# Narrow score tiles of an attention kernel share a PSUM bank and an exponential, and products with V are taken two steps at a time

## The chip, the cores and the metric

The kernel runs on one core of one Trainium2 chip. The metric is the time of one execution on the device, in microseconds (us); every time without a unit in this document is in us. TensorE (PE) multiplies matrices into PSUM, a buffer of 8 banks of 512 fp32 values in each of 128 partitions; ScalarE (ACT) computes exponentials and copies; VectorE (DVE) reduces and adds; GpSimd (POOL) cannot read PSUM and here masks and adds in SBUF; SyncE (SP) issues most transfers.

## The reference

A layer of attention and a layer of a mixture-of-depths feed-forward, each followed by a layer normalisation. Batch 8, 1024 tokens, width 512, 16 heads of 32.

```python
qkv = encodings @ W_attn + b_attn
scores = jnp.einsum('bhki,bhqi->bhkq', k, q) / math.sqrt(HEAD)
mask = jnp.arange(n)[:, None] <= jnp.arange(n)[None, :]
scores = jnp.where(mask, scores, jnp.float32(-10000.0))
attn = jax.nn.softmax(scores, axis=2)
combined = jnp.einsum('bhkq,bhkl->bhql', attn, v)
out = combined.transpose(0, 2, 1, 3).reshape(b, n, HIDDEN) @ W_out + b_out
...
x = _layernorm(x + _L0_attn_ref(x, ...))
x = _layernorm(x + _L0_ffn_ref(x, ...))     # top half of the tokens by score, gelu, scattered back
```

The softmax runs over the key positions `k` that are not after the query position `q`, which makes the scores a triangle.

## The kernel before

The attention part is cut into 64 **units**: for each of 8 batches and 4 groups of 4 heads, the first 512 queries (an even number u, the narrow unit) and the last 512 (an odd number, the wide unit). Two units are a **pair**; there are 32, four to a batch. Each unit passes over its scores twice. Pass A (`a_piece`, line 1287) takes the scores with queries on the partitions, and VectorE (lines 948 and 956) finds the maximum of each query. It is then carried in two extra rows of Q (line 1294 turns the maxima round), so that pass B gives scores that have it subtracted.

Pass B (`b_tile`, line 1318) takes the scores with 128 keys on the partitions: a **step** k is 128 keys, 4 steps in a narrow unit and 8 in a wide one. On the diagonal a step has only the queries from its own keys on, so the last four steps of a unit are 512, 384, 256 and 128 queries wide (`width`). "Step 35.6" below is step 6 of unit 35, which is 256 wide, and 35.7 is 128 wide. A step is four score tiles, one for each head (a to d: 35.3d is the fourth), each in a PSUM bank of its own; two banks, 3 and 4, take turns, so tile j waits until the exponential of tile j-2 has run (semaphore `b_exp`). ScalarE takes one exponential for each tile (line 851) into a buffer of the step: step 0 goes to `acc` (`Pa` in the profile), the others in turn to one of three, `Pm` (two) and `P3` (`P`). From there:

- GpSimd masks the triangle of a diagonal step (line 719, semaphore `keep`) and adds the step to `acc` (line 732, semaphore `padd`); `acc` in the end holds what the sums over all keys are made of. It takes the steps strictly in order.
- TensorE multiplies the step with V (`pv`, line 1334): four heads, each with 32 weight columns and its own 32 output partitions. It waits for the exponentials and, on the diagonal, for `keep`. This is the **product** of the step. `sums`/`N` (line 1261) is a product of the same form that adds `acc` up over the partitions, once in a unit; ScalarE turns it into a reciprocal by a logarithm and an exponential (lines 886 and 888).
- The exponentials of a step wait until the product and the addition of the step three before it are done, since they share its buffer.

Between the tiles TensorE does "dense" work: the projections to K and Q (line 1238) and V (line 1246) for later units, the output projection (line 1252) for earlier tokens. The order is written by a table of **beats** (class `Table`): 32 beats to a pair. Tiles of pass A, tiles of pass B, pieces of dense work and products each have a place in time, and on every engine the order within a beat follows. The table gives the tiles of a unit their places in proportion to a cost for each tile (`168 + 0.87 * width`), and the products of step k a beat two or three behind the one in which the step is formed; the products of the last two steps of a unit stand together. On ScalarE, the copies of projected K and Q (line 869, `nat`) and the conversion of attention outputs (line 895, `Os`) stand behind the exponentials of their beat.

After the attention part the feed-forward runs alone, some 835 us (lines 1368 and 1385); no edit touches it.

## Time and profile before

| | us |
|---|---|
| median of 3 runs | 2638.15 (2637.4 to 2640.35) |
| the profiled execution's own time | 2636.7 |
| its span, first to last instruction | 2634.9 |
| PE with a matmul in flight | 2526.2 (96%) |
| PE loading weights | 1810.5 (69%) |
| DVE busy | 1737.9 (66%) |
| POOL busy | 1518.8 (58%) |
| ACT busy | 1230.9 (47%) |

Times in the profile count from the start of the span. A matmul's record goes from its start to the arrival of its last column and overlaps the next one's, so what a matmul costs is read from start to start. An fp32 product appears as two records for each head, so a step's product is a row of eight. Names in a row are "output<-inputs" without buffer numbers. The mean granted TensorE clock is 0.982.

### The profile page before, as it was taken

The numbers are of one execution on the slowest core, as the hardware profiler recorded it, in microseconds if no ns is written. First come the engines' busy times: TensorE is split into PE (matmuls) and PEld (weight loads), VectorE is DVE, ScalarE is ACT, GpSimd is POOL, SyncE is SP. The second block draws the span as 40 slices with busy tenths as digits, with TensorE's granted clock in tenths as the row PEclk, the third lists the DMA queues.
The fourth block names the chain that finished last, engine by engine and source line by source line (L and its number), as shares of the span: only waits on it lengthen the run. The fifth ranks groups of instructions, "written<-read, shape, count | busy, mean of one in ns | idle before, by whom it ended". The sixth has DMA issues, their size and how long they took to land.

```text
span 2634.9 us, 40165 instructions
## 1 busy us (share of the span) xinstructions
PE 2526.2 (96%) x13920; PEld 1810.5 (69%) x13920; DVE 1737.9 (66%) x4224; ACT 1230.9 (47%) x2342; POOL 1518.8 (58%) x1229
## 2 busy tenths in 40 slices
PE   5999999999999999999999999998899999999997
PEld 4566666666666666666667666665588888888885
DVE  5757678777777877777787677777465435643532
ACT  1555565566565566665565665565631111111110
POOL 0566787687788777778777777876331213122311
PEclk8999999999999999999999999998999999999998
DMA  6766557676666767656666575764431011001000
GB/s 172 127 113 127 101 129 161 125 156 138 137 137 124 164 134 149 154 113 145 126 162 144 124 167 116 141 135 129 160 102 36 25 33 41 17 25 41 29 20 16
DMA packets 167931, 289.57 MB, mean 110 GB/s; under 512 B 23153, under 2 KB 58033, under 8 KB 166578
## 3 DMA queue, kind: packets, MB, share of 16 engines
q1 hardware_dynamic: 160562, 270.15, 47.4%
q0 software_dynamic: 7168, 16.85, 2.0%
q8 instruction: 112, 1.84, 0.3%
q14 instruction: 89, 0.73, 0.1%
HBM read 120.11 MB, written 65.11 MB: 70 GB/s over the span
## 4 chain that ended last, share of the span: by engine, by line
PE 81%; DVE 6%; ACT 4%; POOL 3%; DMA 3%; issue 2%; SPq 1%; ACTq 0%; DVEq 0%; POOLq 0%
PE PS L1385 13%; PE PS L1368 13%; PE PS L1238 10%; PE PS L1318 10%; PE PS L1334 9%; PE PS L1287 9%; PE PS L1252 7%; PE PS L1246 7%; POOL Pa L732 3%; PE PS L1261 2%; DVE xTl L1046 2%; DMA Qp<-nat 1%; DMA h_s<-hs 1%; DVE nm L948 1%; ACT Pm L851 1%
## 5 line engine op out<-in xcount | busy, mean ns | idle before, releaser
L732 POOL TENSOR_TENSOR Pa<-Pa,Pm 128x1024 f32<-128x1024 f32 (+2 forms) x332 | 704.3, 2137 | 168.7 <-ACT Pm L851 119.3
L1318 PE MATMUL PS<-Qp,Kp 98*128 98x512 f32 (+3 forms) x1536 | 548.0, 361 | 16.3 <-ACT P L851 4.6
L851 ACT ACTIVATE Pm<-PS 128x512 f32<-128x512 f32 (+3 forms) x856 | 397.1, 471 | 336.0 <-PE PS L1318 319.7
L1287 PE MATMUL PS<-Kp,Qp 96*128 96x512 f32 (+3 forms) x1536 | 503.9, 363 | 37.8 <-DMA Qp<-nat 18.2
L948 DVE TENSOR_REDUCE nm<-PS 128x1 f32<-128x512 f32 x512 | 345.5, 686 | 223.8 <-PE PS L1287 223.2
L1318 PEld LDWEIGHTS PS<-Qp,Kp 98*128 98x128 f32 x1536 | 293.0, 192 | 220.8 <-ACT Pm L851 92.8
L732 POOL TENSOR_TENSOR Pa<-Pa,P 128x1024 f32<-128x1024 f32 (+2 forms) x164 | 349.3, 2145 | 78.6 <-ACT P L851 55.4
L1287 PEld LDWEIGHTS PS<-Kp,Qp 96*128 96x128 f32 x1536 | 284.0, 194 | 117.3 <-issue 32.5
L820 ACT ACTIVATE G<-PS,b1c 128x512 f32<-128x512 f32 x128 | 88.2, 689 | 539.6 <-PE PS L1368 520.6
L956 DVE CUSTOM_DVE_ANT_0 PS<-PS,maskA 128x384 f32<-128x384 f32 (+3 forms) x512 | 245.3, 505 | 143.5 <-PE PS L1287 141.8
L1385 PE MATMUL PS<-W2h,Gs 128*128 128x512 f32 x1024 | 316.6, 390 | 0.9 <-DVE W2l L1051 0.9
L956 DVE CUSTOM_DVE_ANT_0 PS<-PS,maskA,nm 128x384 f32<-128x384 f32 (+3 forms) x512 | 260.7, 552 | 41.6 <-PE PS L1287 38.4
L1368 PE MATMUL PS<-hT,W1h 128*128 128x512 f32 x1024 | 271.9, 389 | 0.0
L851 ACT ACTIVATE P<-PS 128x512 f32<-128x512 f32 (+3 forms) x424 | 196.6, 469 | 158.3 <-PE PS L1318 148.7
L1098 DVE CAST Gs<-G 128x512 fp32r<-128x512 f32 x128 | 54.4, 425 | 310.1 <-ACT G L820 239.3
L1368 PEld LDWEIGHTS PS<-hT,W1h 128*128 128x128 f32 x1024 | 192.2, 188 | 40.2 <-issue 0.2
L1385 PEld LDWEIGHTS PS<-W2h,Gs 128*128 128x128 f32 x1024 | 191.1, 188 | 40.2 <-issue 1.3
L771 POOL TENSOR_SCALAR rs<-mv 128x1 f32<-128x1 f32 x32 | 9.8, 307 | 347.1 <-DVE mv L1082 345.0
L1238 PE MATMUL PS<-xTh,Wkh 128*128 128x512 f32 x512 | 184.7, 407 | 23.4 <-DVE Wkl L1034 14.2
L1238 PE MATMUL PS<-xTh,Wkl 128*128 128x512 f32 x512 | 202.0, 424 | 0.0
L851 ACT ACTIVATE Pa<-PS 128x512 f32<-128x512 f32 x256 | 151.9, 598 | 102.2 <-PE PS L1318 99.3
L1385 PE MATMUL PS<-W2l,Gs 128*128 128x512 f32 x512 | 199.3, 389 | 0.0
(139 smaller groups left out, 4343.8 us busy)
## 6 DMA issues: line engine op xcount, KB each, us to landing
Kp<-nat SPq DMA_DIRECT2D x192, 256.0 KB, 6.1
Qp<-nat SPq DMA_DIRECT2D x192, 256.0 KB, 6.6
x_raw<-in_xt SPq DMA_DIRECT2D x16, 1024.0 KB, 6.1
o_s<-Of SPq DMA_DIRECT2D x64, 256.0 KB, 2.1
Ot<-o_s SPq DMA_DIRECT2D x64, 256.0 KB
xb<-in_x SPq DMA_DIRECT2D x64, 256.0 KB, 3.5
h_s<-hs SPq DMA_DIRECT2D x64, 256.0 KB, 3.7
out<-xb SPq DMA_DIRECT2D x64, 256.0 KB, 3.6
```

Source lines behind the costliest of these rows:

```text
L732: e.tensor_tensor(to, to, tile[:, h0:h0 + many, 0:w], ALU.add).then_inc(s["padd"], many // 2)
L851: e.activation(probs(u, k)[:, h_, 0:w], PS[:, B_BANKS[j % 2], 0:w], ACT.Exp).then_inc(s["b_exp"], 1)
L948: ins = e.tensor_reduce(out=nm[:, u % 2, 0, hh[0], qt:qt + 1], in_=PS[:, A_BANKS[j % 3], :], op=ALU.max, axis=AX, negate=True)
L956: ins = e.tensor_tensor_reduce(out=to, in0=to, in1=maskA[:, 512 - w:512], scale=-1.0, scalar=least, op0=ALU.add, op1=ALU.min, accum_out=nm ...
L1238: ins = e.matmul(to, Wk[wh][:, 1 if kind == "K" else 0, kt, :], xT[xh][:, kt, c * 512:c * 512 + 512], start=k == 0, stop=k == 11)
L1246: ins = e.matmul(to[:, t * 256:t * 256 + 256], xT[xh][:, kt, tok:tok + P], Wv[wh][:, kt, :], start=m == 0, stop=m == 11)
L1252: ins = e.matmul(to, Os[:, oh, kt, :], Wo[wh][:, kt, :], start=k == 0, stop=False)
L1287: ins = e.matmul(to, Qp[0:96, u % 4, h_, qt * P:qt * P + P], Kp[0:96, (2 * i + k0 // 512) % 4, h_, 0:w], start=True, stop=True)
L1318: e.matmul(PS[:, B_BANKS[j % 2], 0:w], Kp[0:98, (2 * i + k // 4) % 4, h_, k % 4 * P:k % 4 * P + P], Qp[0:98, u % 4, h_, 512 - w:512], star ...
L1334: ins = e.matmul(PO[32 * h_:32 * h_ + 32, 512 - w:512], V[:, (u // 4 * 4 + k // 2) % 6, k % 2, vo:vo + HD], probs(u, k)[:, h_, 0:w], start ...
L1368: ins = e.matmul(PS[:, UP_BANKS[j % 2], :], W1p[wh][k][:, f * P:f * P + P], hT[:, xh, k, :], start=n_ == 0, stop=n_ == 11)
L1385: ins = e.matmul(PS[:, DOWN_BANK + t, :], Gs[:, j % 3, gh, t * P:t * P + P], W2p[wh][f // 4][:, f % 4, :], start=f == 0 and n_ == 0, stop= ...
```

## The change

Pass B's tiles are grouped. A step of width 256 has its four heads in two tiles of two heads, and a step of width 128 in one tile of four; each tile fills a bank (2 x 256 or 4 x 128 columns) and gets one exponential, which writes 2 or 4 pieces of its buffer. Wider steps keep a tile for each head. All matmuls stay, with the same shapes. The counting of tiles follows (`tiles_of`, `tiles_before`: 38 in a pair instead of 48), and the table's places are computed for the new tiles: each of them costs `168 + 0.87 * width * heads`, so the places of the unchanged wide tiles move too.

In the wide unit, products are now listed in groups (`PRODUCTS`): 0, then 1 with 2, 3 with 4, 5, and 6 with 7. A group stands where its last step's product would. Before, only 6 and 7 stood together. In the narrow unit the groups are as before.

```diff
+PRODUCTS = (((0,), (1,), (2, 3)), ((0,), (1, 2), (3, 4), (5,), (6, 7)))
...
-def tiles_before(u):
-    return 4 * ksteps_before(u)
+def tiles_of(u, k):
+
+    w = width(u, k)
+    return [(0, 1, 2, 3)] if w == P else [(0, 1), (2, 3)] if w == 2 * P else [(h_,) for h_ in range(HG)]
+
+
+def tiles_before(u, k=0):
+    return 38 * (u // 2) + 11 * (u % 2) + sum(len(tiles_of(u, x_)) for x_ in range(k))
...
-            work = [168 + 0.87 * width(u, t // 4) for t in range(4 * ksteps(u))]
-            for t in range(4 * ksteps(u)):
+            some = [(k, hh) for k in range(ksteps(u)) for hh in tiles_of(u, k)]
+            work = [168 + 0.87 * width(u, k) * len(hh) for k, hh in some]
+            for t, (k, hh) in enumerate(some):
                 p = u // 2 * 2 * BEATS + at + (end - at) * sum(work[:t]) / sum(work)
-                self.tiles.setdefault(int(p), []).append((p, (u, t // 4, t % 4)))
-                self.formed[u, t // 4] = int(p)
-            last = ksteps(u) - 1
+                self.tiles.setdefault(int(p), []).append((p, (u, k, hh)))
+                self.formed[u, k] = int(p + (end - at) * work[t] / sum(work) * (1 - 1 / len(hh)))
+
             for k in range(ksteps(u)):
-                n = self.formed[u, max(k, last) if k == last - 1 else k] + (2 if diag(u, k) is None else 3)
+                k1 = max([g for g in PRODUCTS[u % 2] if k in g][0])
+                n = self.formed[u, k1] + (2 if diag(u, k1) is None else 3)
...
-                    e.activation(probs(u, k)[:, h_, 0:w], PS[:, B_BANKS[j % 2], 0:w], ACT.Exp).then_inc(s["b_exp"], 1)
+                    e.activation(probs(u, k)[:, hh[0]:hh[-1] + 1, 0:w],
+                                 PS[:, B_BANKS[j % 2], 0:len(hh) * w].rearrange("p (h n) -> p h n", n=w),
+                                 ACT.Exp).then_inc(s["b_exp"], 1)
...
-                e.matmul(PS[:, B_BANKS[j % 2], 0:w], Kp[0:98, (2 * i + k // 4) % 4, h_, k % 4 * P:k % 4 * P + P],
-                         Qp[0:98, u % 4, h_, 512 - w:512], start=True, stop=True).then_inc(s["b_mm"], 1)
+                for x_, h_ in enumerate(hh):
+                    ins = e.matmul(PS[:, B_BANKS[j % 2], x_ * w:x_ * w + w],
+                                   Kp[0:98, (2 * i + k // 4) % 4, h_, k % 4 * P:k % 4 * P + P],
+                                   Qp[0:98, u % 4, h_, 512 - w:512], start=True, stop=True)
+                ins.then_inc(s["b_mm"], 1)
```

TensorE's order of before, from the sums of unit 34 (the first row; 32 output rows and 512 columns) through the product of step 35.2 (second product row) to tile 35.3d, the score tile (L1318) right behind it. L1287 is pass A, L1238 a projection.

```order
L1261 MATMUL PS<-Pa,ones 32x512 x4
L1318 MATMUL PS<-Qp,Kp 128x512
L1287 MATMUL PS<-Kp,Qp 128x512
L1334 MATMUL PS<-Pm,V 32x512 x4
L1318 MATMUL PS<-Qp,Kp 128x512
L1238 MATMUL PS<-xTh,Wkh 128x512 x2
```

The same place after the change, in which L1274, L1332, L1350, L1300 and L1251 are the old L1261, L1318, L1334, L1287 and L1238; tiles 35.3b and 35.3c stand between the sums and the products, the products are those of 35.1 and 35.2, and the last row is tile 35.3d.

```order
L1274 MATMUL PS<-Pa,ones 32x512 x4
L1332 MATMUL PS<-Qp,Kp 128x512
L1300 MATMUL PS<-Kp,Qp 128x512
L1332 MATMUL PS<-Qp,Kp 128x512
L1350 MATMUL PS<-P,V 32x512 x4
L1350 MATMUL PS<-Pm,V 32x512 x4
L1251 MATMUL PS<-xTh,Wkh 128x512 x2
L1300 MATMUL PS<-Kp,Qp 128x512
L1332 MATMUL PS<-Qp,Kp 128x512
```

The product of 35.1 has moved here from before the sums, and tile 35.3d is three matmuls further behind the products. The second place is TensorE's order after the change from the first half of step 35.6 to step 35.7: the products of 35.3 and 35.4 stand together between the two halves of step 35.6, and step 35.7 is four matmuls in a row.

```order
L1332 MATMUL PS<-Qp,Kp 128x256 x2
L1251 MATMUL PS<-xTh,Wkh 128x512 x2
L1350 MATMUL PS<-Pm,V 32x512 x4
L1350 MATMUL PS<-P,V 32x512 x4
L1300 MATMUL PS<-Kp,Qp 128x384
L1251 MATMUL PS<-xTh,Wkh 128x512
L1332 MATMUL PS<-Qp,Kp 128x256 x2
L1251 MATMUL PS<-xTh,Wkl 128x512
L1300 MATMUL PS<-Kp,Qp 128x384
L1251 MATMUL PS<-xTh,Wkl 128x512 x2
L1332 MATMUL PS<-Qp,Kp 128x128 x4
```

Before, the product of 35.3 stood between tiles 35.4c and 35.4d, and that of 35.4 behind the first tile of 35.6. ScalarE's order around the end of unit 35, before (L851 is the exponential, L869 the copy of a projection, L895 the conversion):

```order
L851 ACTIVATE Pm<-PS 128x256 x3
L869 ACTIVATE nat<-PS,battn 128x512
L895 ACTIVATE Os<-Ot 128x512
L851 ACTIVATE Pm<-PS 128x256
L851 ACTIVATE P<-PS 128x128 x4
```

And after the change, where L862, L882 and L908 are the same three:

```order
L862 ACTIVATE Pm<-PS 128x2x256
L882 ACTIVATE nat<-PS,battn 128x512
L908 ACTIVATE Os<-Ot 128x512
L862 ACTIVATE Pm<-PS 128x2x256
L862 ACTIVATE P<-PS 128x4x128
```

Eight exponentials have become three, with the copy and the conversion still between the halves of step 35.6. The orders of VectorE and SyncE are the same before and after, and so is GpSimd's in the attention part but for one place in the last units.

## Rows read from the trace of the kernel before

**Rows 1.** The page's chain that ended last: shares of the span by engine.
```profile
PE 81%; DVE 6%; ACT 4%; POOL 3%; DMA 3%; issue 2%; SPq 1%; ACTq 0%; DVEq 0%; POOLq 0%
```

**Rows 2.** Windows, ordinary pair, batch change: us, busy PE PEld DVE ACT POOL, PEclk, DMA.
```profile
1034.50:1089.60 55.10, 54.87 (x336) 37.43 (x340) 39.63 (x103) 33.37 (x66) 42.41 (x32) 1.00 0.65 126
1117.80:1177.70 59.90, 55.97 (x337) 37.36 (x336) 48.03 (x109) 35.08 (x69) 44.70 (x33) 1.00 0.60 122
```

**Rows 3.** Timeline, PE, tiles 35.3d to 35.4d. Start, length, engine, line, operation.
```profile
1065.34 0.50 PE L1318 MATMUL PS<-Qp,Kp 98*128 98x512 f32 x1
...
1068.94 0.63 PE L1238 MATMUL PS<-xTl,Wkh 128*128 128x512 f32 x2
1069.51 1.06 PE L1334 MATMUL PS<-Pm,V 128*32 128x512 f32 x8
1070.50 0.50 PE L1287 MATMUL PS<-Kp,Qp 96*128 96x512 f32 x1
1070.84 0.40 PE L1238 MATMUL PS<-xTl,Wkh 128*128 128x512 f32 x1
1071.07 0.40 PE L1318 MATMUL PS<-Qp,Kp 98*128 98x512 f32 x1
```

**Rows 4.** Timeline, PE, steps 35.7's tiles and products of 35.5 to 35.7.
```profile
1079.72 0.40 PE L1238 MATMUL PS<-xTh,Wkl 128*128 128x512 f32 x1
1080.22 0.33 PE L1318 MATMUL PS<-Qp,Kp 98*128 98x128 f32 x1
1080.47 0.85 PE L1334 MATMUL PS<-Pm,V 128*32 128x384 f32 x8
1081.26 0.50 PE L1238 MATMUL PS<-xTh,Wkl 128*128 128x512 f32 x1
...
1082.11 0.23 PE L1318 MATMUL PS<-Qp,Kp 98*128 98x128 f32 x1
...
1082.46 0.34 PE L1287 MATMUL PS<-Kp,Qp 96*128 96x384 f32 x1
...
1086.23 0.64 PE L1334 MATMUL PS<-Pm,V 128*32 128x256 f32 x8
1086.71 0.43 PE L1334 MATMUL PS<-P,V 128*32 128x128 f32 x8
1087.07 0.51 PE L1252 MATMUL PS<-Woh,Os 128*128 128x512 f32 x1
```

**Rows 5.** Timeline, PE, behind the sums of unit 35.
```profile
1090.85 0.64 PE L1287 MATMUL PS<-Kp,Qp 96*128 96x128 f32 x4
1091.33 0.39 PE L1318 MATMUL PS<-Qp,Kp 98*128 98x384 f32 x1
1091.56 0.63 PE L1238 MATMUL PS<-xTh,Wkh 128*128 128x512 f32 x2
1092.33 0.44 PE L1318 MATMUL PS<-Qp,Kp 98*128 98x384 f32 x1
```

**Rows 6.** Timeline, ACT, the end of step 35.6.
```profile
1079.26 0.63 ACT L895 ACTIVATE Os<-Ot 128x512 fp32r<-128x512 f32 x1
1079.78 0.39 ACT L851 ACTIVATE Pm<-PS 128x256 f32<-128x256 f32 x1
```

**Rows 7.** Groups by form: a copy that writes 4 pieces of 128.
```profile
L809 ACT ACTIVATE hT<-PS 128x512 fp32r<-128x512 f32 x28 | 15.2, 596 | 16.7 <-PE PS L1350 16.7
```

**Rows 8.** Timeline, POOL: addition of 35.3, masks of 35.4, 35.5 and 35.7.
```profile
1067.29 4.74 POOL L732 TENSOR_TENSOR Pa<-Pa,Pm 128x1024 f32<-128x1024 f32 x2
1072.17 0.64 POOL L719 TENSOR_SCALAR_AFFINE_SELECT P<-P 128x512 f32<-128x512 f32 x1
...
1077.58 1.10 POOL L719 TENSOR_SCALAR_AFFINE_SELECT Pm<-Pm 128x512 f32<-128x512 f32 x1
...
1085.93 0.63 POOL L719 TENSOR_SCALAR_AFFINE_SELECT P<-P 128x512 f32<-128x512 f32 x1
```

**Rows 9.** Timeline, DVE: the product with the router's weights.
```profile
1075.61 2.57 DVE L1158 CUSTOM_DVE_ANT_0 hs<-hs,wrB 128x512 f32<-128x512 f32 x1
```

More of the change, by code:

```diff
@@ L228, in streams @@
             at, end = B_AT[u % 2]
[L229 to L230 removed]
+            some = [(k, hh) for k in range(ksteps(u)) for hh in tiles_of(u, k)]
+            work = [168 + 0.87 * width(u, k) * len(hh) for k, hh in some]
+            for t, (k, hh) in enumerate(some):
                 p = u // 2 * 2 * BEATS + at + (end - at) * sum(work[:t]) / sum(work)
[L232 to L234 removed]
+                self.tiles.setdefault(int(p), []).append((p, (u, k, hh)))
+                self.formed[u, k] = int(p + (end - at) * work[t] / sum(work) * (1 - 1 / len(hh)))
             for k in range(ksteps(u)):
[L236 removed]
+                k1 = max([g for g in PRODUCTS[u % 2] if k in g][0])
+                n = self.formed[u, k1] + (2 if diag(u, k1) is None else 3)
+                assert not by_products(u) or n < self.beat["N", u]
                 self.products.setdefault(n, []).append((u, k))
@@ L269, in steps_formed @@
     def steps_formed(self, n):
-        return [x[:2] for x in self.score_tiles(n) if x[2] == 3]
+        return [x[:2] for x in self.score_tiles(n) if x[2][-1] == HG - 1]
     def pv_steps(self, n):
@@ L465, in tiles_read @@
         def tiles_read(u, k):
-            return s["b_mm"], tiles_before(u) + 4 * k
+            return s["b_mm"], tiles_before(u, k)
         def formed(u, k):
-            return s["b_exp"], tiles_before(u) + 4 * k + 4
+            return s["b_exp"], tiles_before(u, k + 1)
         last_x = max(T.x_users[B - 1, c] for c in range(2))
@@ L833, in scalar @@
                     split_v(0)
-                for u, k, h_ in T.score_tiles(n):
-                    j = tiles_before(u) + 4 * k + h_
+                for u, k, hh in T.score_tiles(n):
+                    j = tiles_before(u, k) + tiles_of(u, k).index(hh)
                     w = width(u, k)
                     e.wait_ge(s["b_mm"], j + 1)
-                    if h_ == 0:
+                    if hh[0] == 0:
                         a = added(u, k)
@@ L1308, in ring_entry, with b_tile @@
                     a_piece(j, *x_[1:])
-            def b_tile(u, k, h_):
+            def b_tile(u, k, hh):
                 i, c = u // 2, u % 2
-                j = tiles_before(u) + 4 * k + h_
+                j = tiles_before(u, k) + tiles_of(u, k).index(hh)
                 w = width(u, k)
-                if k == 0 and h_ == 0:
+                if k == 0 and hh[0] == 0:
                     e.wait_ge(s["shift"], 32 * (u + 1))
```

## The prediction

> **What bounds the kernel now.** I read the chain that ended last first: TensorE holds 81% of it, no other engine over 6% [rows 1]. So a microsecond counts where TensorE loses it. The table of windows then shows how the attention part runs. An ordinary pair of units takes 55.10 us, TensorE has matmuls in flight for 54.87 of them at clock 1.00, ScalarE is busy for 33.4 and GpSimd for 42.4; a pair in which the batch changes takes 59.90, and there VectorE's load rises from 39.6 to 48.0 [rows 2]. Matmul records overlap, so "busy" hides short waits; I read TensorE's list in time for the distances from start to start. A plain 512-wide matmul takes 0.23 (1070.84 to 1071.07) [rows 3].
>
> Two things stand out against that 0.23. Before the second 128-wide score tile of unit 35 the distance is 0.50 (1079.72 to 1080.22), and after the sums two projections and their wait take 0.77 (1091.56 to 1092.33) where 0.47 would do: 0.27 and 0.30 lost [rows 4, 5]. ScalarE shows the first cause: the exponential that frees the bank runs at 1079.78, behind the conversion at 1079.26 [rows 6].
>
> The third thing is GpSimd. It masks step 35.4 at 1072.17 and step 35.7 at 1085.93, with no pause between; the second mask ends at 1086.56 [rows 8], and TensorE's product for step 35.7 starts at 1086.71, 0.48 after that of step 35.6 (1086.23) [rows 4]: 0.15 after the mask. GpSimd is exactly in step with TensorE there. I take its slack as zero: whatever makes GpSimd later against TensorE becomes a wait.
>
> **The change, part by part.** A pair has 48 exponentials before and 38 after; the number of matmuls is the same. *Exponentials.* The wide unit's end needs 3 instead of 8. The merged form writes a 4x128 pattern; the nearest row with such an output is the turned copy, 596 ns [rows 7], so I take 0.60 for each. ScalarE is not the bound; it matters only at the two waits. The first goes: after the change only one exponential (35.6, first half) stands between the bank's turn and its next use, some 1.7 us ahead of it. With it goes about 0.03 that the next product loses behind a narrow tile (1080.22 to 1080.47 is 0.25, where 0.12 for the tile, below, and 0.10 for going in would do [rows 4]): 0.30 in all. The second stays. ScalarE now runs no 384-wide exponential ahead of the sums; the first of them comes behind logarithm and reciprocal, and the third tile waits for it instead of the fourth: 0.30 before and after.
>
> *Products.* A group of its own costs more than its columns. A 512-wide step takes 0.99 (1069.51 to 1070.50), a 384-wide one 0.79 (1080.47 to 1081.26): 0.20 to 0.21 for each 128 columns, so 0.15 to 0.17 is fixed. Two projections before it take 0.57 where 0.47 is usual, 0.10 more for going in [rows 3, 4]. Two steps of 256 and 128 in one group take 0.84 (1086.23 to 1087.07), against 0.79 for the same columns in one step: a second step costs 0.05 [rows 4]. Fixed 0.15 and 0.10 less 0.05 is 0.20; some of it is already overlapped in the exit, so 0.19 for each merge, two in a pair: 0.38. Bounds: 0.10 (only the entry) and 0.25.
>
> *Narrow tiles in a row.* After the 128-wide tile at 1082.11 the next two starts span 0.35 (a tile and a 512-wide projection, so 0.12 for the tile); four 128-wide ones in a row take 0.48, 0.12 each [rows 4, 5]. Clustering them costs nothing. The Trainium skill ("TensorE: Matmul & The Clock Gate", LDWEIGHTS) says a weight load takes the weight's columns at 1.2 GHz, here 107 ns, twice what 128 moving columns stream in; taken alone it says that scattered tiles hide their loads and clustered ones expose them, about 0.05 for three tiles in each unit, 10 us in all: 2634. The rows above show the scattered ones paying already.
>
> *Where the steps stand now.* The order shows step 35.1's product moved from before the sums of unit 34 to behind them, with 35.2's; step 35.3's from between tiles 35.4c and 35.4d to a group with 35.4's between the two halves of 35.6. Score tile 35.3d, which used to stand right behind the product of 35.2, now has another tile, another step and three matmuls ahead of it. Against the sums of unit 34 it is later by 0.82+0.05 for the step, 0.23 for the tile, and 3 matmuls of which the first takes 0.34 (1070.50 to 1070.84 [rows 3]): 0.81. Sum 1.91: from 1065.34 to 1067.25. GpSimd can take up a step 1.10 after the start of its last tile (1071.07, where it was waiting, to 1072.17 [rows 3, 8]), so here at 1068.35.
>
> GpSimd adds step 35.3 from 1067.29 to 1072.03 [rows 8]; it was not waiting for the tile, but was busy until then. Now it starts at 1068.35, 1.06 later, and its 4.74 end at 1073.09. Tile 35.4d comes 19 starts after 35.3d, 1067.25 + 19 x 0.234 = 1071.70, and is formed by 1072.80, so the mask follows directly: at 1073.09 and not at 1072.17, 0.92 later, as the gap of 0.14 ahead of it is gone. From there to the end of the last mask GpSimd needs 1072.17 to 1086.56, 14.39, unbroken. So the last mask ends 0.92 later, at 1087.48.
>
> TensorE reaches the product of step 35.7 later too, by less: plus 0.87 (step 35.1), plus 0.23 (the tile that stood before the sums), minus 0.19 (the merge of 35.3 and 35.4; that of 35.1 is in the 0.87), minus 0.30 (the ScalarE wait): 0.61. **It waits 0.92 - 0.61 = 0.31.** Its bounds are 0, if the addition finds its step formed in time, and 1.2, if GpSimd stays bound by its own work alone for all of the 1.91. A wait of ScalarE is added, too: the first exponential of 35.6 waits for the product of 35.3, which used to be long done. Queued behind it are the copy of Q, the conversion and the second half of 35.6. The product of 35.3 starts near 1077.45 and ends 1.06 later; that exponential is done by 1079.2, and TensorE wants its bank for step 35.7 only near 1080.9. ScalarE is through with all four, 0.6 each, by 1081.1, and the bank of the second half is wanted in the next unit. Hidden; if TensorE were at 35.7 before 1079.2 it would wait up to 0.6, an exponential, in each pair.
>
> *Sum.* In a pair in step with GpSimd: -0.38 - 0.30 + 0.31 = -0.37. I count 25 of 32 as such, -9.3 us. In the 7 others (six changes of batch and the last pair) the pair is 4.8 longer for TensorE [rows 2], GpSimd is done in time, and the 0.68 stays, -4.8; bounds there are 0, as TensorE waits for VectorE in that stretch anyway, and -1.1, as a step and a tile (0.87 and 0.23) move into that wait. The feed-forward part has none of it. Sum -14.1 on the profiled execution's 2636.7, 2622.6; that run is 1.45 below the median of the runs, 2638.15, so 2624.05 there. I say 2624.
>
> **Rivals.** *GpSimd keeps up* (its last mask is no later against TensorE than before, because the addition of 35.3 is not held by the tile, or a mask gets shorter; masks take 0.64 at 1072.17 and 1.10 at 1077.58 [rows 8]). Then 25 x 0.31 = 8 more: 2616. For it: that spread, and a wait small against the terms it is the difference of. Against it: GpSimd has no slack now.
> *GpSimd gets slower, and the kernel with it.* The mask of 1.10 stands where VectorE's product with the router's weights, both inputs in SBUF, runs from 1075.61 for 2.57 [rows 8, 9]. If GpSimd's later place meets two more such operations, at 0.46 each, TensorE waits 1.23 in place of 0.31: 25 x 0.92 = 23 us more, 2647. The kernel is slower by 5.3 from a wait of 0.68 + (5.3 + 4.8) / 25 = 1.08 on. The Trainium skill ("SBUF — State Buffer", Who interferes with whom) has such a mechanism: a VectorE instruction with two SBUF inputs contends with a GpSimd one that reads SBUF, and the loser blocks; the spread of the masks agrees. Against it: the chain of 14.39 meets such an operation already, and moving both only changes which instruction pays.
> *The ScalarE wait only moves* (behind the product of 35.3, or behind the sums, where it may grow): 0.30 x 32 = 10 are not won, 2634.
> *Clustered narrow tiles cost.* By its columns a 128-wide tile would take 0.06, a quarter of 0.23, and a row shows 0.12; if scattered ones hid the other 0.06 and clustered ones did not, three tiles in each of 64 units would cost 11 more, 2635. Against it: the 0.12 of the scattered one.
>
> **How the numbers follow.** Forecast 0.45, GpSimd keeps up 0.23, GpSimd slower 0.17, ScalarE's wait moves 0.12, clustered tiles 0.03. The forecast's own terms (merge 0.10 to 0.25, batch changes 0 to -1.1, the wait by 0.2 either way) spread it from 2614 to 2635. A measurement here can tell 0.2%, 5.3 us, from no change. Faster is what lies below 2632.9: about 0.39 of the forecast's 0.45 and all of the next case, 0.62. The two cases near 2635 and the forecast's rest lie within 0.2%, and of the slow case a little: 0.23. Slower 0.15. The range 2612 to 2641 leaves out most of the slow rival and a low tail.
>
> **What would show it.** After the change: 1216 exponentials in place of 1536; one distance fewer above 0.3 ahead of the last score tile of the wide unit; the mask of 35.4 directly behind the addition of 35.3; the product of 35.7 some 0.8 behind that of 35.6, not 0.48; ordinary pairs at 54.7. The forecast is wrong if that distance stays 0.48 (GpSimd keeps up) or exceeds 1.5 (GpSimd slower), or if an exponential of the wide unit's end holds TensorE elsewhere.

## The result, and the profile after

The changed kernel takes 2644.08 us (median of 20 runs) against 2634.39 for the kernel before (20 runs beside them): the ratio is 1.0037, 95% interval 1.0027 to 1.0048. It is slower by 0.37%, some 10 us, where 14 us less were forecast; 2644.08 lies above the predicted range. Its profiled execution has a span of 2640.1 us at a mean clock of 0.982, against 2634.9 at 0.982.

The page of the changed kernel, span and busy times, and the chain that ended last by engine and by line:

```profile
span 2640.1 us, 39845 instructions
PE 2507.3 (95%) x13920; PEld 1813.6 (69%) x13920; DVE 1736.1 (66%) x4224; ACT 1176.4 (45%) x2022; POOL 1524.9 (58%) x1229
PE 58%; POOL 25%; DVE 8%; issue 5%; ACT 3%; DMA 2%; SPq 0%; POOLq 0%; DVEq 0%; ACTq 0%
POOL Pa L743 21%; PE PS L1401 13%; PE PS L1384 13%; PE PS L1259 6%; PE PS L1350 6%; PE PS L1332 5%; PE PS L1300 4%; PE PS L1251 4%; DVE xTl L1059 3%; PE PS L1265 3%; DVE nm L961 2%; POOL Pm L730 2%; PE PS L1274 1%; DMA Qp<-nat 1%; ACT Pm L862 1%
```

In [rows 1] TensorE held 81% of the chain and GpSimd 3%. Now GpSimd holds 25%, nearly all of it in its additions (L743). GpSimd is busy for no more than 58%; the chain says that in the attention part TensorE's waits now lead back to it.

Three stretches of the changed kernel in windows: an ordinary pair of units, from the product of step 33.7 to that of 35.7, and the last 40 us in which the last pair runs (columns as in [rows 2]):

```profile
1027.20:1082.30 55.10, 54.24 (x335) 37.84 (x336) 39.33 (x102) 31.62 (x56) 42.48 (x33) 1.00 0.61 126
...
1840.00:1860.00 20.00, 12.44 (x64) 4.33 (x68) 8.74 (x10) 14.55 (x24) 12.26 (x13) 0.78 0.33 95
1860.00:1880.00 20.00, 17.43 (x100) 9.32 (x96) 5.54 (x10) 9.20 (x17) 2.67 (x6) 0.79 0.23 77
```

The same last stretches of the kernel before:

```profile
1840.00:1860.00 20.00, 15.00 (x108) 5.92 (x108) 8.79 (x11) 17.32 (x31) 12.67 (x15) 1.00 0.28 82
1860.00:1880.00 20.00, 17.75 (x120) 10.04 (x120) 7.36 (x12) 12.01 (x26) 3.83 (x9) 1.00 0.31 94
```

ScalarE's load in the ordinary pair falls from 33.37 [rows 2] to 31.62. The last pair is where the clock falls from 1.00 to 0.78 and 0.79, that is, TensorE spends a part of those stretches at 1.2 GHz, and it does so behind gaps: in the first of them it is busy for 12.44 of 20 us, where it was 15.00. From the product of step 61.7 to the feed-forward part the mean clock is 0.84 against 0.93 before.

In what follows "a pair" is the distance, start to start, from one product of step 7 to that of the next odd unit. From the product of 9.7 to that of 59.7 there are 25 of them, 19 ordinary and 6 with a change of batch. Before, the 19 sum to 1048.29 (55.17 each) and the 6 to 367.77 (61.3); after, 1045.34 (55.02) and 371.38 (61.9). So the ordinary pairs won 2.95, the batch changes lost 3.61, together +0.66. The start up to 9.7 won 3.7. The pair up to 61.7 lost 0.95 (61.32 to 62.27), and from there to the feed-forward part it takes 60.7 instead of 53.5, 7.2 more. These make +5.1 of the span's +5.2. So more of the loss stands in the batch changes and at the end than in the ordinary pairs: against the forecast of -0.37 for each ordinary pair the 19 lack 4 us, and where the forecast had -4.8 for the batch changes and the last pair together, they lost 11.8.

TensorE in the changed kernel at the products of 35.6 and 35.7:

```profile
1080.65 0.39 PE L1265 MATMUL PS<-Woh,Os 128*128 128x512 f32 x1
1080.97 0.64 PE L1350 MATMUL PS<-Pm,V 128*32 128x256 f32 x8
1082.28 0.42 PE L1350 MATMUL PS<-P,V 128*32 128x128 f32 x8 [0.67 <-POOL P L730]
```

The product of 35.7 starts 1.31 behind that of 35.6, 0.48 before [rows 4] and 0.8 forecast: where nothing waits there the distance is 0.46 (in the experiments with that product later), so the wait is about 0.85 in each ordinary pair, not 0.31. Its releaser is the last mask. GpSimd in the changed kernel, from the addition of step 35.1 to the last mask:

```profile
1051.77 4.75 POOL L743 TENSOR_TENSOR Pa<-Pa,P 128x1024 f32<-128x1024 f32 x2 [6.61 <-ACT P L862]
1056.67 4.71 POOL L743 TENSOR_TENSOR Pa<-Pa,Pm 128x1024 f32<-128x1024 f32 x2
1061.46 0.19 POOL L751 TENSOR_SCALAR lnrs<-lnmv 128x1 f32<-128x1 f32 x1
...
1063.04 4.76 POOL L743 TENSOR_TENSOR Pa<-Pa,Pm 128x1024 f32<-128x1024 f32 x2
1067.73 0.66 POOL L730 TENSOR_SCALAR_AFFINE_SELECT P<-P 128x512 f32<-128x512 f32 x1
...
1081.50 0.64 POOL L730 TENSOR_SCALAR_AFFINE_SELECT P<-P 128x512 f32<-128x512 f32 x1
```

And the start of the same work in the kernel before:

```profile
1055.44 4.73 POOL L732 TENSOR_TENSOR Pa<-Pa,P 128x1024 f32<-128x1024 f32 x2 [5.75 <-ACT P L851]
1060.92 4.72 POOL L732 TENSOR_TENSOR Pa<-Pa,Pm 128x1024 f32<-128x1024 f32 x2 [0.74 <-ACT Pm L851]
```

These times must be set against TensorE's. TensorE's timeline of the changed kernel, tile 35.1d (the last of its step) and the sums of unit 34, and then the same two rows of the kernel before:

```profile
1050.61 0.40 PE L1332 MATMUL PS<-Qp,Kp 98*128 98x512 f32 x1
...
1057.03 1.07 PE L1274 MATMUL PS<-Pa,ones 128*32 128x512 f32 x8
```

```profile
1054.29 0.39 PE L1318 MATMUL PS<-Qp,Kp 98*128 98x512 f32 x1
...
1062.69 1.06 PE L1261 MATMUL PS<-Pa,ones 128*32 128x512 f32 x8
```

Tile 35.1d stood 8.40 ahead of the sums and now stands 6.42 ahead, 1.98 later. GpSimd takes up step 35.1 at 1.16 behind that tile, so 5.26 ahead of the sums instead of 7.25. Before, it then paused 0.74 for step 35.2. Now nothing pauses from 35.1 to the last mask: the addition of 35.3 starts 6.01 behind the sums (before 4.60), 1.41 later, and the last mask ends 25.11 behind them (before 23.87), 1.24 later.

### The profile page after: what moved, and what is told of

It is laid out like the page before. It is cut to its first block, busy times and chain, and to the rows that moved or that the text cites. A ratio compares the mean times of both kernels' runs of the same rounds, so it can differ in the third digit from the quotient of the medians.

```text
span 2640.1 us, 39845 instructions
## 1 busy us (share of the span) xinstructions
PE 2507.3 (95%) x13920; PEld 1813.6 (69%) x13920; DVE 1736.1 (66%) x4224; ACT 1176.4 (45%) x2022; POOL 1524.9 (58%) x1229
## 4 chain that ended last, share of the span: by engine, by line
PE 58%; POOL 25%; DVE 8%; issue 5%; ACT 3%; DMA 2%; SPq 0%; POOLq 0%; DVEq 0%; ACTq 0%
POOL Pa L743 21%; PE PS L1401 13%; PE PS L1384 13%; PE PS L1259 6%; PE PS L1350 6%; PE PS L1332 5%; PE PS L1300 4%; PE PS L1251 4%; DVE xTl L1059 3%; PE PS L1265 3%; DVE nm L961 2%; POOL Pm L730 2%; PE PS L1274 1%; DMA Qp<-nat 1%; ACT Pm L862 1%
## 5 line engine op out<-in xcount | busy, mean ns | idle before, releaser
L743 POOL TENSOR_TENSOR Pa<-Pa,Pm 128x1024 f32<-128x1024 f32 (+2 forms) x332 | 718.2, 2179 | 158.3 <-ACT Pm L862 126.3
L1300 PE MATMUL PS<-Kp,Qp 96*128 96x512 f32 (+3 forms) x1536 | 497.9, 359 | 42.2 <-DVE nm L961 19.6
L1332 PE MATMUL PS<-Qp,Kp 98*128 98x512 f32 (+3 forms) x1536 | 497.2, 362 | 15.2 <-ACT Pm L862 5.7
L862 ACT ACTIVATE Pm<-PS 128x512 f32<-128x512 f32 (+1 forms) x643 | 358.6, 569 | 310.0 <-PE PS L1332 243.8
L961 DVE TENSOR_REDUCE nm<-PS 128x1 f32<-128x512 f32 x512 | 344.9, 686 | 193.1 <-PE PS L1300 192.9
L743 POOL TENSOR_TENSOR Pa<-Pa,P 128x1024 f32<-128x1024 f32 (+2 forms) x164 | 356.6, 2190 | 72.9 <-ACT P L862 57.1
L1332 PEld LDWEIGHTS PS<-Qp,Kp 98*128 98x128 f32 x1536 | 280.9, 192 | 157.3 <-issue 38.0
L1300 PEld LDWEIGHTS PS<-Kp,Qp 96*128 96x128 f32 x1536 | 281.2, 191 | 138.9 <-DVE nm L969 35.9
L969 DVE CUSTOM_DVE_ANT_0 PS<-PS,maskA,nm 128x384 f32<-128x384 f32 (+3 forms) x512 | 266.4, 554 | 96.5 <-PE PS L1300 93.3
L862 ACT ACTIVATE P<-PS 128x512 f32<-128x512 f32 (+1 forms) x317 | 176.7, 570 | 147.3 <-PE PS L1332 113.7
L862 ACT ACTIVATE Pa<-PS 128x512 f32<-128x512 f32 x256 | 152.0, 598 | 152.0 <-PE PS L1332 149.1
L1251 PE MATMUL PS<-xTh,Wkh 128*128 128x512 f32 x512 | 185.4, 416 | 25.7 <-DVE Wkl L1047 14.1
L1350 PE MATMUL PS<-Pm,V 128*32 128x512 f32 (+3 forms) x1712 | 172.6, 490 | 13.1 <-POOL Pm L730 13.1
```

The source lines that it names most:

```text
L743: e.tensor_tensor(to, to, tile[:, h0:h0 + many, 0:w], ALU.add).then_inc(s["padd"], many // 2)
L862: e.activation(probs(u, k)[:, hh[0]:hh[-1] + 1, 0:w], PS[:, B_BANKS[j % 2], 0:len(hh) * w].rearrange("p (h n) -> p h n", n=w), ACT.Exp).th ...
L961: ins = e.tensor_reduce(out=nm[:, u % 2, 0, hh[0], qt:qt + 1], in_=PS[:, A_BANKS[j % 3], :], op=ALU.max, axis=AX, negate=True)
L969: ins = e.tensor_tensor_reduce(out=to, in0=to, in1=maskA[:, 512 - w:512], scale=-1.0, scalar=least, op0=ALU.add, op1=ALU.min, accum_out=nm ...
L1251: ins = e.matmul(to, Wk[wh][:, 1 if kind == "K" else 0, kt, :], xT[xh][:, kt, c * 512:c * 512 + 512], start=k == 0, stop=k == 11)
L1300: ins = e.matmul(to, Qp[0:96, u % 4, h_, qt * P:qt * P + P], Kp[0:96, (2 * i + k0 // 512) % 4, h_, 0:w], start=True, stop=True)
```

## The experiments

Ratios are to the kernel before, timed beside each. The pair is the median of the ordinary ones in the steady stretch (16 in the kernel before, 14 to 16 elsewhere); "end" is from product 61.7 to the feed-forward part.

| kernel | products | narrow tiles | places of tiles | 35.7 | median us | ratio [95%] | pair | end |
|---|---|---|---|---|---|---|---|---|
| before | single | single | old | as is | | 1 | 55.14 | 53.5 |
| changed | merged | shared | new | as is | 2644.08 | 1.0037 [1.0027, 1.0048] | 55.02 | 60.7 |
| e1 | single | shared | new | as is | 2658.82 | 1.0103 [1.0089, 1.0118] | 55.98 | 60.4 |
| e2 | merged | single | old | as is | 2623.38 | 0.9963 [0.9951, 0.9975] | 54.47 | 55.1 |
| e3 | merged but last pair | shared | new | as is | 2643.07 | 1.0037 [1.0024, 1.0051] | 54.94 | 59.4 |
| e4 | merged | shared | new | later | 2628.83 | 0.9987 [0.9977, 0.9998] | 54.15 | 61.5 |
| e5 | merged | shared | old | as is | 2619.85 | 0.9943 [0.9924, 0.9962] | 54.41 | 55.5 |
| e6 | merged | single | new | as is | 2670.18 | 1.0129 [1.0109, 1.0149] | 55.73 | 62.6 |
| e7 | single | shared | old | as is | 2632.52 | 0.9990 [0.9978, 1.0002] | 55.16 | 54.4 |
| e8 | merged | shared | old, new in last pair | as is | 2627.36 | 0.9969 [0.9957, 0.9981] | 54.44 | 61.0 |
| e9 | merged | shared | old | later | 2611.81 | 0.9914 [0.9899, 0.9929] | 54.19 | 56.7 |
| e10 | merged | shared | old, wide ones earlier | as is | 2777.37 | 1.0535 [1.0516, 1.0555] | 60 to 62 | 53.8 |
| e13 | single | shared | old | later | 2625.79 | 0.9956 [0.9941, 0.9972] | 54.83 | 51.3 |
| e14 | merged | single | old | later | 2617.00 | 0.9930 [0.9909, 0.9950] | 54.45 | 54.7 |

My first theory (A) was: the ordinary pairs win little because GpSimd's chain ends late, and the last pair's merged products and sums cost the 8 us. The rivals were that the shared tiles cost (B), and that the wait behind the last mask is all of it (C). The first four kernels put them apart.

**e1, the tiles alone.**

```diff
-PRODUCTS = (((0,), (1,), (2, 3)), ((0,), (1, 2), (3, 4), (5,), (6, 7)))
+PRODUCTS = (((0,), (1,), (2, 3)), ((0,), (1,), (2,), (3,), (4,), (5,), (6, 7)))
```

> The tiles of the change alone: 128-wide and 256-wide score tiles share banks and exponentials, every step's product stands where its own formation puts it (no merged pair but that of the last two steps). Theory A (the ordinary pairs gain little because GpSimd's chain ends against TensorE about 0.5 later than before, the batch-change pairs gain nothing, and the last pair loses some 8 us where merged products and sums hold back ScalarE): here nothing moves GpSimd's start, and the last pair has no merged products, so the ScalarE wait of 0.30 goes in each pair and nothing comes back: 25 to 32 times 0.30, 7 to 10 us faster than the kernel before, ratio 0.996 to 0.9975; product 35.7 still about 0.5 (at most 0.8) behind product 35.6. Theory B (the shared tiles themselves cost: narrow tiles in a row, or an exponential that now frees a bank later): slower than before or the same, ratio 1.000 to 1.005.

It is slower by 1.03%. Theory A missed by more than 30 us, in the pairs and in the last pair: the end loses its 7 us with no merged product. TensorE at products 35.6 and 35.7 of this kernel:

```profile
1091.32 0.64 PE L1350 MATMUL PS<-Pm,V 128*32 128x256 f32 x8
1092.91 0.43 PE L1350 MATMUL PS<-P,V 128*32 128x128 f32 x8 [0.95 <-POOL P L730]
```

The distance is 1.59: the wait for the mask is there, and longer, though here no merge delays a tile.

**e2, the merged products alone.**

```diff
-    return [(0, 1, 2, 3)] if w == P else [(0, 1), (2, 3)] if w == 2 * P else [(h_,) for h_ in range(HG)]
+    return [(h_,) for h_ in range(HG)]
...
-    return 38 * (u // 2) + 11 * (u % 2) + sum(len(tiles_of(u, x_)) for x_ in range(k))
+    return 48 * (u // 2) + 16 * (u % 2) + sum(len(tiles_of(u, x_)) for x_ in range(k))
```

> The merged products of the change alone: every score tile holds one head again. Theory A: GpSimd's chain sets the end of an ordinary pair, so the ScalarE wait of 0.30 that comes back is taken out of the wait for the last mask (0.85 in the changed kernel, here about 0.5), and the ordinary pairs are as in the changed kernel, 0.1 to 0.2 shorter than before; the last pair still loses about 8 us. Ratio 1.002 to 1.005. Theory B (the shared tiles cost): the merges are worth 0.38 in each pair with at most 0.3 lost, so faster than before, ratio below 0.998.

Faster by 0.37%, pairs 0.67 shorter, no wait ahead of 35.7 (the mask ends at 24.32 behind the sums, the product comes at 24.53). So the merges are good and the tiles' part is bad. Theory A falls. But "the tiles" are two edits: banks and exponentials are shared, and the spread of the tiles over the beats weighs a shared tile as 168 + 0.87 x its columns, once, where four single ones weighed 168 four times. With narrow tiles that light, every wide tile of the unit stands later. In the table tile 35.1d stands at 41.94 beats from the start of its pair with the old weights and at 42.23 with the new ones, so it has gone over into the next beat. That is theory D, tried from e5 on.

**e3, the last pair's products single.**

```diff
+LONE = (((0,), (1,), (2, 3)), ((0,), (1,), (2,), (3,), (4,), (5,), (6, 7)))
...
-                k1 = max([g for g in PRODUCTS[u % 2] if k in g][0])
+                k1 = max([g for g in (LONE if by_products(u) else PRODUCTS)[u % 2] if k in g][0])
```

> The changed kernel, but in the last pair of units (62 and 63) each step of the wide unit but the last two has its product and its sums by itself, as before the change. Theory A: the start of the feed-forward part comes 7 to 8 us earlier against product 61.7 than in the changed kernel, TensorE is at half clock there for 17 us less, and the ratio to the kernel before is 0.999 to 1.001 (the changed kernel 1.0037). Theory C (the cost is the wait behind the last mask, 0.85 in each of 25 pairs, and the last pair's loss is chance of the clock): within 2 us of the changed kernel, ratio 1.003 to 1.0045.

The ratio is that of the changed kernel, and the end takes 59.4: of 7.2 lost, the merges make 1.3 at these places.

**e4, the product of 35.7 one beat later.**

```diff
-                n = self.formed[u, k1] + (2 if diag(u, k1) is None else 3)
+                n = self.formed[u, k1] + (2 if diag(u, k1) is None else 3) + (1 if k1 == 7 and not by_products(u) else 0)
```

> The changed kernel, but the product of steps 6 and 7 of the wide unit is issued one beat later (not in the last pair), so that the last mask has about 1.4 us more to be done. Theory C (the wait of 0.85 in front of product 35.7 is what costs): the wait goes and nothing takes its place, 25 times 0.5 to 0.85, 12 to 21 us faster than the changed kernel, ratio to before 0.996 to 0.999. Theory A: TensorE and GpSimd take the same time for a pair; the wait goes from this place, and what GpSimd is late by is found again at its next meeting with TensorE (the next units' products or sums), except for what slack there is: 3 to 12 us faster than the changed kernel at most, ratio 0.999 to 1.003. If the ratio stays at 1.0037 with no wait here, GpSimd's own work bounds the pair.

Pairs fall from 55.02 to 54.15, by 0.87, the whole wait; 15 us come back, as theory C had it for this place. GpSimd's lateness does not come up anywhere else: its next meeting with TensorE has room. The end stays at 61.5, so that part has another cause than this product.

**e5, e6 and e7, the places apart from the sharing.** e5 is the changed kernel with the old weights, in narrow and wide units, e6 is e2 with the new ones, e7 is e5 with single products (and the `PRODUCTS` of e1).

```diff
-            work = [168 + 0.87 * width(u, k) * len(hh) for k, hh in some]
+            work = [(168 + 0.87 * width(u, k)) * len(hh) for k, hh in some]
```

```diff
-            work = [168 + 0.87 * width(u, k) * len(hh) for k, hh in some]
+            work = [168 * {P: 1, 2 * P: 2}.get(width(u, k), 4) / 4 + 0.87 * width(u, k) for k, hh in some]
```

> The changed kernel, but a shared tile weighs as much as its heads weighed apart when the wide unit's tiles are spread over the beats, so that every tile stands in the beat that it had before the change (35.1d some 0.8 earlier against the sums of unit 34 than in the changed kernel); banks, exponentials and merged products are those of the changed kernel. Theory D (the cost is in the places: a shared tile weighs less in the spread, so all wide tiles ahead of it move back, GpSimd's additions start later and its last mask ends too late for product 35.7): GpSimd takes up step 35.1 at 6.1 before the sums of unit 34 and not at 5.25, product 35.7 starts 0.5 behind product 35.6 with no wait, an ordinary pair takes 54.47 - 0.30 = 54.15 to 54.2, the end of the attention part is as with the merged products alone; ratio to the kernel before 0.991 to 0.994. Theory B (the sharing itself costs, by its exponentials or by narrow tiles in a row): pairs stay at 55.0, the ratio at 1.002 to 1.004.

> Nothing shared: every score tile holds one head with its own bank and exponential, the products are merged as in the changed kernel, but the tiles are spread over the beats by the weights of the changed kernel (narrow ones light, all others later). Theory D: the wait in front of product 35.7 comes back without any shared tile, 0.5 to 0.85, an ordinary pair takes about 55.0 (54.47 with the old places), the last pair loses its 5 to 7 us; ratio 1.002 to 1.005. Theory B: as with the merged products alone, 0.995 to 0.998.

> Shared tiles at the old places, products not merged: the sharing by itself against the kernel before. Theory D: only the first ScalarE wait goes, an ordinary pair takes 55.13 - 0.30 = 54.8, nothing is lost in the last pair; ratio 0.995 to 0.998 (at the new places this kernel was at 1.0103 with pairs of 55.98). Theory B: 1.005 or more.

e5 gives back all of it and more: one pair of brackets in the order's weights turns 1.0037 into 0.9943. TensorE's timeline of e5, with tile 35.1d, the sums of unit 34 and the products of 35.6 and 35.7, and GpSimd's, with the addition of 35.1 and the last mask:

```profile
1046.38 0.39 PE L1332 MATMUL PS<-Qp,Kp 98*128 98x512 f32 x1
...
1053.59 1.06 PE L1274 MATMUL PS<-Pa,ones 128*32 128x512 f32 x8
...
1077.36 0.64 PE L1350 MATMUL PS<-Pm,V 128*32 128x256 f32 x8
1078.03 0.43 PE L1350 MATMUL PS<-P,V 128*32 128x128 f32 x8
```

```profile
1047.53 4.75 POOL L743 TENSOR_TENSOR Pa<-Pa,P 128x1024 f32<-128x1024 f32 x2 [5.79 <-ACT P L862]
...
1077.25 0.63 POOL L730 TENSOR_SCALAR_AFFINE_SELECT P<-P 128x512 f32<-128x512 f32 x1
```

The tile stands 7.21 ahead of the sums, 0.79 earlier than in the changed kernel; the addition starts 0.80 earlier (6.06 ahead), and the last mask ends 24.29 behind the sums, 0.82 earlier (25.11 in the changed kernel). The shift of one tile arrives at the far end of GpSimd's chain undiminished. Product 35.7 now starts 0.67 behind 35.6, 0.15 behind the mask's end: a small wait is left, which is why the pair is 54.41 and not the 54.15 expected.

e6 has no shared tile and is the slowest of the three, 1.0129: the new places alone do the harm, as theory D expects, and more than it expected. The wait for the mask is back (0.46 in its row), and a second one comes up, shown here in TensorE's row of e6 behind the four 128-wide tiles of step 34.3 (1055.33 to 1056.38):

```profile
1056.38 0.23 PE L1332 MATMUL PS<-Qp,Kp 98*128 98x128 f32 x1
1057.11 0.47 PE L1332 MATMUL PS<-Qp,Kp 98*128 98x512 f32 x1 [0.51 <-ACT Pm L862]
...
1100.32 0.32 PE L1350 MATMUL PS<-P,V 128*32 128x128 f32 x4 [0.46 <-POOL P L730]
```

In that row single exponentials, with the copy of a projection between them, do not keep up with narrow tiles that stand this close together; in the changed kernel, with one shared exponential at the same place, the wait is not there. At the new places sharing is worth 0.71 a pair (55.73 to 55.02), at the old ones 0.06 (54.47 to 54.41).

e7 has pairs of 55.16, no shorter than before. Expected were 54.8. TensorE comes to product 35.6 at 23.23 behind the sums instead of 23.54, so the 0.31 of ScalarE's wait is won there; the product of 35.7 then starts at 0.14 behind a mask that ends when it always did. What ScalarE gave, GpSimd took. Its ratio, 0.9990, is not clear of 1.

**e8, new places in the last pair only.**

```diff
-            work = [(168 + 0.87 * width(u, k)) * len(hh) for k, hh in some]
+            work = [(168 + 0.87 * width(u, k)) * len(hh) if not by_products(u) else 168 + 0.87 * width(u, k) * len(hh) for k, hh in some]
```

> The kernel with shared tiles, merged products and the old places, but in the last pair of units alone the tiles stand where the changed kernel has them. If the places make the last pair's loss too: from product 61.7 to the feed-forward part 60 to 61.5, against 55.5 with the old places throughout, ratio 0.996 to 0.9975, ordinary pairs unchanged at 54.4. If the last pair's loss comes from pairs before it, or from chance of the clock: 55 to 56.5 and a ratio of 0.994 to 0.995.

The end takes 61.0 instead of 55.5, the ratio goes from 0.9943 to 0.9969. So the places make the last pair's loss as well, most of it: at the old places the end of e5 still takes 2.0 more than before, behind a pair up to 61.7 that is 1.6 shorter. One window from product 61.7 to the feed-forward part in e8, and one in e5:

```profile
1808.42:1869.39 60.97, 51.39 (x284) 23.65 (x276) 25.19 (x50) 36.12 (x61) 22.74 (x28) 0.78 0.27 85
```

```profile
1808.12:1863.60 55.48, 49.04 (x283) 23.76 (x276) 26.05 (x50) 35.73 (x61) 22.68 (x28) 0.83 0.26 79
```

With the same work, e8 has TensorE at a mean clock of 0.78 and not 0.83; an estimate from these shares is 27 us at 1.2 GHz against 19. Of the 5.5 us, 2.3 are longer busy time and 3.1 are time without a matmul (9.6 against 6.4). The longest single wait in this stretch of the changed kernel and of e8 is the one ahead of the first product of unit 63. That product and what ScalarE did before it, in the changed kernel, and the product in e8 and in e5:

```profile
1848.18 1.94 PE L1350 MATMUL PS<-Pa,V 128*32 128x512 f32 x8 [4.73 <-ACT Pm L862]
```

```profile
1844.61 0.81 ACT L917 ACTIVATE hs<-xb,lnnb,lnrs 128x512 f32<-128x512 f32 x1 [3.03 <-POOL lnnb L758]
...
1847.45 0.58 ACT L871 ACTIVATE Of<-PS 128x512 f32<-128x512 f32 x1
```

```profile
1829.90 1.93 PE L1350 MATMUL PS<-Pa,V 128*32 128x512 f32 x8 [3.31 <-ACT Of L871]
```

```profile
1830.26 1.94 PE L1350 MATMUL PS<-Pa,V 128*32 128x512 f32 x8 [0.50 <-ACT Of L871]
```

In all three the product starts 0.14 to 0.15 behind the end of ScalarE's copy of unit 62's output (L871), which empties the bank that the product writes. That copy is queued behind a layer norm (L917), and the layer norm waits for GpSimd's short operations: for 3.03 in the changed kernel, 1.61 in e8, and not at all in e5. Before, the same product waited 1.59. How the later tiles bring ScalarE to wait for GpSimd there was not tried.

**e9, e13 and e14, product 35.7 one beat later at the old places** (the edit of e4, on e5, e7 and e2).

> Old places, shared tiles, merged products, and product 35.7 one beat later, not in the last pair. Theory D with GpSimd as the pace of the ordinary pair at product 35.7: the wait that still stands there (0.54 minus 0.41 behind the last mask) goes too, the pair falls from 54.41 to 54.15, the level that TensorE's own work sets in the run with that product later; ratio 0.991 to 0.993. If TensorE's own work already sets 54.41, nothing changes: 0.994 to 0.995.

> Shared tiles at the old places, products not merged, product 35.7 one beat later (not in the last pair). If the 0.30 that the first ScalarE wait gives back was taken by the wait for GpSimd's last mask (pairs of 55.16 with that product at its old beat, against 55.14 in the kernel before), it shows here: pairs of 54.85 to 54.9, ratio 0.995 to 0.997. If the sharing costs elsewhere what it gives, pairs stay at 55.1, ratio 0.998 to 1.000.

> Merged products, nothing shared, old places, product 35.7 one beat later (not in the last pair). TensorE came to that product after the last mask already (24.56 against 24.32 behind the sums), so nothing is to be had: pairs of 54.4 to 54.5, ratio 0.9955 to 0.997. If pairs fall to 54.2, the product's later place itself is worth the 0.28 and not the sharing.

With that wait out of the way each part shows its worth in pairs: sharing 0.31 alone (55.14 to 54.83) and 0.26 with the merges (54.45 to 54.19), the merges 0.69 alone and 0.64 with sharing. They add up. e9 is the fastest, 0.9914, faster than the kernel before by 0.86%, with a median 32 us under the changed one's. e14's ratio is better than expected though its pairs are as expected: it is 3.9 us ahead of e2 at product 9.7 already. Start-ups differ by such amounts between these kernels, from 346.6 in the changed one to 356.7 in e6 at product 9.7. Where two kernels have the same order there, they agree better, to 0.4 (the changed kernel and e3) and 1.3 (e5 and e8), so such a difference belongs to the order at the start and says nothing of the ordinary pairs. Some 0.15% of a ratio can come from it, as 3.7 of the 7.9 us by which e9's span is below e5's; the pairs are the surer measure. The ends in the table are to be read with this care too: e13's 51.3 stands behind a pair up to 61.7 that takes 65.5, where it was 61.3 before.

**e10, narrow tiles that weigh more.**

```diff
-            work = [(168 + 0.87 * width(u, k)) * len(hh) for k, hh in some]
+            work = [(168 + 0.87 * width(u, k)) * len(hh) * (1.5 if u % 2 and len(hh) > 1 and not by_products(u) else 1) for k, hh in some]
```

> Old places but for the shared tiles of the wide unit, which weigh 1.5 times as much in the spread (not in the last pair), so that all 512-wide and 384-wide tiles stand earlier; sharing and merges as in the changed kernel. Theory D: GpSimd takes up step 35.1 earlier still against the sums, the last mask is done before TensorE comes to product 35.7, an ordinary pair takes 54.1 to 54.3, ratio 0.991 to 0.9935. If the sums of unit 34 or the bank of the shared tile become the limit instead, 54.5 or more and a ratio above 0.995.

A clear miss: 5.35% slower. Wide tiles that stand earlier do bring GpSimd to step 35.1 earlier (6.55 ahead of the sums), and then this happens, in rows of ScalarE, GpSimd and TensorE:

```profile
1140.37 0.60 ACT L862 ACTIVATE P<-PS 128x512 f32<-128x512 f32 x1 [0.33 <-PE PS L1332]
1145.17 0.81 ACT L917 ACTIVATE hs<-xb,lnnb,lnrs 128x512 f32<-128x512 f32 x1 [4.21 <-POOL lnnb L758]
```

```profile
1138.70 4.75 POOL L743 TENSOR_TENSOR Pa<-Pa,Pm 128x1024 f32<-128x1024 f32 x2 [0.87 <-ACT Pm L862]
1143.53 0.19 POOL L751 TENSOR_SCALAR lnrs<-lnmv 128x1 f32<-128x1 f32 x1
...
1144.87 0.27 POOL L758 TENSOR_SCALAR lnnb<-lnrs,lnmv 128x2 f32<-128x2 f32 x1
```

```profile
1147.22 0.69 PE L1332 MATMUL PS<-Qp,Kp 98*128 98x384 f32 x1 [4.14 <-ACT P L862]
1147.71 0.63 PE L1251 MATMUL PS<-xTh,Wkh 128*128 128x512 f32 x1
1148.14 0.63 PE L1300 MATMUL PS<-Kp,Qp 96*128 96x512 f32 x1
```

In the changed kernel the four short operations of the layer norm (L751 to L758) come between the additions of 35.2 and 35.3. Here the addition of 35.3 stands ahead of them; ScalarE waits for their result with the exponentials queued behind, and TensorE waits for a bank. The window right behind that wait:

```profile
1147.50:1152.00 4.50, 4.50 (x13) 3.82 (x14) 2.04 (x3) 2.10 (x5) 4.42 (x3) 0.50 0.16 62
```

TensorE's granted clock is 0.50 there. The pair grows by 5 to 7 us. So tiles 0.8 us later cost a wait of 0.85 in the pair, and this edit, with 35.1d at 7.71 ahead of the sums and so 0.5 earlier than in e5, a wait of 4. Earliness by itself is not the harm, since the kernel before had that tile at 8.40; what differs is where the layer norm stands among the additions.

## Why the prediction was wrong

**The failed step** is "GpSimd adds step 35.3 from 1067.29 to 1072.03 [rows 8]; it was not waiting for the tile, but was busy until then. Now it starts at 1068.35, 1.06 later". I asked when step 35.3 is formed and took GpSimd's own earlier work as unmoved. The tile came where I had it, 1.89 later against the sums (1.91 forecast), but GpSimd was still busy and took it up 0.35 after it could have. For the tiles had moved since the start of the unit: 35.1d was 1.98 later against the sums (of which e2 shows that the merges make 1.2, 8.40 to 7.22, and the new places the other 0.8), and from the addition of 35.1 on GpSimd had only one pause, of 0.74, to absorb it in. What arrives at 35.3 is 1.41. The last mask is 1.24 later, not 0.92, and the wait 0.85, not 0.31. I had written that the places of all the wide tiles move, and reckoned with it at 35.3d alone; the order beside the trace would have shown 35.1d as well as it showed 35.3d. e5 and e6 undo and make this one thing, and move the wait and the ratio with it.

**A second step failed, and by its size it weighs more:** "In the 7 others (six changes of batch and the last pair) ... GpSimd is done in time, and the 0.68 stays, -4.8". GpSimd is in time there: the last mask of unit 37 ends 2.28 ahead of its product, before 2.76. But the new places were put at nothing, and in these pairs they cost through other waits. The six changes of batch lost 3.6, the pair up to 61.7 1.0 and the end 7.2, together 11.8 us instead of 4.8 won; against e5, which has the old places, that is 8.5, 2.5 and 5.2. The signs that I had named for a wrong forecast (a distance of 0.48, or above 1.5) did not show it: 1.31 lies between, and they look at the ordinary pair alone.

**The merges** were under-sized: 0.19 each by my sum, above the bound of 0.25 too, 0.32 to 0.35 measured. Two parts were in hand. With 0.20 for each 128 columns, the difference of the two steps, the fixed part is 0.19 and not the 0.15 that I took. And the first matmul behind a group takes 0.34 and not 0.23, 1070.50 to 1070.84 in [rows 3], 0.11 for going out; I counted that as time that tile 35.3d is later and not in the price of a group. The merged pair itself starts 1.86 ahead of the next dense matmul (1058.91 to 1060.77), as summed: 0.99 and 0.87.

**TensorE's own lateness at 35.7** was less: 0.40 instead of 0.61 (product 35.6 at 23.94 behind the sums, before 23.54). Most of the difference is what the merge gives more. 1.24 less 0.40 is the 0.84 of the wait.

**What was foreseen:** there are 1216 exponentials (643, 317 and 256 of L862), and the mask of 35.4 stands directly behind the addition of 35.3 (1067.73, where the addition ends at 1067.80 by its record). The ScalarE waits were right: the first goes and is worth 0.26 to 0.31 (e9, e13), the second stays. **The exponential of 35.6 behind product 35.3** waits 1.99 and is hidden, as said. **Narrow tiles in a row** cost nothing: the pair of e13 is shorter by all of the 0.31. By the rate for weight loads in the Trainium skill ("TensorE: Matmul & The Clock Gate", LDWEIGHTS) my estimate was 0.05 for each clustered tile; no run here shows such a cost.

**GpSimd slower by collisions**, the rival with the right sign, was not what happened: from mask 35.4 to the end of the last mask it takes 14.41 (1067.73 to 1082.14), 14.39 before, though different instructions are the long ones. The wait of 0.85 comes near the 1.08 from which that rival makes the kernel slower, but it comes from a later start and not from slower work.

**The batch changes** were to win 0.68 each and lost 0.6. In e5 they take 60.5 against 61.3 before, 0.8 won (60.2 in e8, whose order is the same there): the size was about right for the parts, and the new places took it and more. **The last pair** was counted among them and lost 7.2 at its end; e8 shows the same cause for 5.5 of them.

In sum, e5 against the changed kernel (both profiled) says what the places cost: 11.5 in the 19 ordinary pairs (1045.34 less 1033.86), 8.5 in the 6 batch changes (371.38 less 362.92), 2.5 in the pair up to 61.7 and 5.2 at the end, less 5.0 by which the changed kernel's start is ahead: 22.7, where the spans differ by 22.6. The sharing and the merges without the move are faster by 0.57%; with it, slower by 0.37%. In the last pair the traces point at one wait, the 4.73 ahead of the first product of unit 63. In the batch changes none stands out: from product 35.7 to 37.7 TensorE waits for VectorE for 4.0 in all (2.3 for the maxima, L961, and 1.7 for L1059), where it is 3.6 before and 2.3 in e5, and its mean clock is 0.95, against 1.00 and 0.97. Which of them the later tiles lengthen stays open.

## What to carry to other kernels

When an edit changes the costs by which an order is spread, all of that order moves, not only what was edited: compare the order at the first place where a near-bound engine starts an unbroken run of work, not where its result is due. An engine that runs unbroken from there passes a shift on undiminished, and its few pauses are the only slack. Where two engines are in step, the gain of one edit is taken by the other engine's wait until that due point is moved too: the 0.3 of the shared exponentials showed as 0.06 or as nothing, and as 0.26 to 0.31 once product 35.7 stood a beat later.
